# Cross-attention with a sparse feed-forward on one core: the feed-forward stage of the last group taken a step later

## The reference, cut to what matters

```
def _L0_xattn_ref(...):            # 32 query heads in 8 groups of 4, D = 128
    q, k, v = query @ Wq, key @ Wk, value @ Wv     # then rotary embedding on q and k
    attn = jax.nn.softmax(jnp.where(mask == 0, -1e9, q @ k.T / sqrt(D)), axis=-1)
    return (attn @ v) @ Wo

def _L0_ffn_ref(hidden_states, router_weight, router_bias, expert_bias):
    logits = jnp.einsum('th,eh->te', flat, router_weight) + router_bias
    scores = jax.nn.softmax(logits, axis=-1)       # 64 experts
    topk_w, topk_idx = jax.lax.top_k(scores, 8)
    w_sum = topk_w.sum(axis=-1, keepdims=True)
    w_dense = zeros.at[rows, topk_idx].add(topk_w)
    return flat * w_sum + w_dense @ expert_bias

x = x + _L0_xattn_ref(_layernorm(x), ctx, ctx, ...)
x = x + _L0_ffn_ref(_layernorm(x), ...)
```

## Time and profile before

| | |
|---|---|
| Median of 3 runs | 610.95 us (610.76 to 611.58) |
| The profiled execution | 615.61 us, its span 613.7 us |
| Busy in the span | PE 586.2 us (96%), DVE 479.1 (78%), POOL 423.8 (69%), ACT 396.0 (65%) |
| Granted clock of PE | 0.985 of full over the span; 0.7 in the last of 40 slices |
| Chain that ended last, by engine | PE 68%, DVE 9%, POOL 7%, issue 6%, ACT 5%, DMA 3% |

### The profile page before, as it was taken

The page is one execution under the profiler, slowest core; times in us unless marked ns, Lnnn a source line. Parts: engine busy times, 40 slices in busy tenths (PEclk is TensorE's granted clock), DMA queues, the critical chain, the costliest instruction groups (busy, mean ns, idle before and its releaser), DMA issues.

```text
span 613.7 us, 10554 instructions
## 1 busy us (share of the span) xinstructions
PE 586.2 (96%) x2980; PEld 490.4 (80%) x2980; DVE 479.1 (78%) x792; ACT 396.0 (65%) x1054; POOL 423.8 (69%) x390
## 2 busy tenths in 40 slices
PE   8989889898999999999999999999999999999886
PEld 7867778677888888888888888888888888777674
DVE  5667986777778687877977798778787876977886
ACT  5236454767767777677776777767767776775443
POOL 5466588879687787868868886787787763664231
PEclk9989999998999999999999999999999999999997
DMA  8965324210321301121012111111310030000001
GB/s 289 347 186 138 97 104 152 88 35 15 107 68 36 88 23 64 51 85 51 17 52 85 51 51 49 54 68 34 102 36 33 17 86 18 19 18 1 36 34 71
DMA packets 30817, 45.40 MB, mean 74 GB/s; under 512 B 3008, under 2 KB 11328, under 8 KB 30784
## 3 DMA queue, kind: packets, MB, share of 16 engines
q1 hardware_dynamic: 30256, 43.95, 22.6%
q0 software_dynamic: 384, 1.05, 0.5%
q10 hardware_dynamic: 144, 0.00, 0.0%
HBM read 35.03 MB, written 9.96 MB: 73 GB/s over the span
## 4 chain that ended last, share of the span: by engine, by line
PE 68%; DVE 9%; POOL 7%; issue 6%; ACT 5%; DMA 3%; SPq 2%; DVEq 0%; ACTq 0%; POOLq 0%
PE outp L1614 8%; PE score L1595 8%; PE outp L1616 8%; PE outp L1615 8%; PE bank_a L1467 4%; PE bank_a L1469 4%; PE bank_a L1468 4%; PE probT L1627 4%; POOL rot L495 3%; DMA v_dram<-v_stage 2%; PE attnT L1453 2%; PE bank_c L1469 2%; PE bank_c L1468 2%; PE attnT L1455 2%; PE attnT L1454 2%
## 5 line engine op out<-in xcount | busy, mean ns | idle before, releaser
L495 POOL TENSOR_TENSOR rot<-rot,sinT 128x512 f32<-128x512 f32 x80 | 110.5, 1382 | 51.4 <-ACT rot L742 51.2
L908 ACT ACTIVATE probs<-score,negmax 128x128 f32<-128x128 f32 x256 | 90.7, 367 | 29.2 <-DVE negmax L1241 29.2
L615 POOL TENSOR_TENSOR probs<-probs,rsum 128x512 f32<-128x512 f32 x64 | 69.3, 1083 | 45.6 <-DVE rsum L1247 45.6
L1614 PE MATMUL outp<-wo_hi,oT_hi 128*128 128x512 f32 x240 | 95.5, 398 | 2.1 <-DVE oT_lo L1266 1.3
L1616 PE MATMUL outp<-wo_hi,oT_lo 128*128 128x512 f32 x240 | 93.8, 391 | 0.0
L1615 PE MATMUL outp<-wo_lo,oT_hi 128*128 128x512 f32 x240 | 93.5, 390 | 0.0
L1254 DVE TENSOR_TENSOR resid<-resid,outp 128x512 f32<-128x512 f32 x60 | 41.0, 684 | 54.4 <-PE outp L1616 54.4
L1093 DVE TENSOR_TENSOR qT<-qT,rot 128x512 f32<-128x512 f32 x57 | 69.9, 1230 | 4.0 <-POOL rot L495 1.6
L1595 PEld LDWEIGHTS score<-kT,qT 128*128 128x128 f32 x512 | 67.6, 193 | 5.5 <-DVE qT L1093 0.6
L1595 PE MATMUL score<-kT,qT 128*128 128x128 f32 x512 | 68.3, 277 | 0.2 <-DVE qT L1093 0.2
L916 ACT ACTIVATE pT_hi<-probT 128x512 fp32r<-128x512 f32 x64 | 38.3, 598 | 42.2 <-PE probT L1627 41.8
(11 more groups left out here) (297 smaller groups left out, 1513.2 us busy)
## 6 DMA issues: line engine op xcount, KB each, us to landing
ring_b<-in_wo SPq DMA_DIRECT2D x32, 256.0 KB
ring_a<-in_wq SPq DMA_DIRECT2D x28, 256.0 KB, 2.7
v_dram<-v_stage SPq DMA_DIRECT2D x16, 256.0 KB, 3.5
v_raw<-v_dram SPq DMA_DIRECT2D x16, 256.0 KB, 2.6
k_dram<-k_stage SPq DMA_DIRECT2D x14, 256.0 KB, 2.1
kT<-k_dram SPq DMA_DIRECT2D x14, 256.0 KB, 2.8
ctx_in<-in_ctx SPq DMA_DIRECT2D x8, 256.0 KB, 4.1
ring_b<-in_wv SPq DMA_DIRECT2D x8, 256.0 KB
```

What stands on the lines that cost most here:

```text
L495: pool.tensor_tensor(rot[:, k0 % 2, :], rot[:, k0 % 2, :], sinT[:, half * W:(half + 1) * W], ALU.mult).then_inc(sin_done, 1)
L615: pool.tensor_tensor(probs[:, p], probs[:, p], rsum[:, p, :].unsqueeze(2).broadcast_to([P, GH, S]), ALU.mult).then_inc(soft_done, 1)
L908: last = act.activation(probs[:, p, h, :], heads(score[p][:, :])[:, h, :], ACT.Exp, bias=negmax[:, p, h:h + 1], accum_out=sums[:, p, h:h + 1])
L1614: pe.matmul(ps[:, :], oT_hi[:, cols], w[0], start=h == 0, stop=False)
```

## The change

The feed-forward is the same, instruction for instruction; the last group's order changes on PE, DVE, ACT and POOL, three instructions of blocks 0 to 4 go from DVE to POOL, and banks are dealt out otherwise.

- PE: ffn_logits(b-3) stands between the scores and the transposes of step b, one step later than before; the kept transpose is that of block b-4 and stands ahead of output; ffn_mix is that of block b-4 at the step's end. ffn_xT stays where it was.
- DVE: ffn_max(b-3) and, from step 5, ffn_out(b-5) come behind lo_p. After accumulate the order is invert_sums, ffn_keep(b-3), ffn_stats(b-1), lo_o.
- ACT: the exponentials of the attention come ahead of ffn_exp(b-3) and ffn_xT(b-2).
- POOL: soften comes ahead of the feed-forward's part, and a new ffn_split(b-3) does ff_kept and ff_split for blocks 0 to 4.
- Block 4 mixes in score[0]; the logits of block 6 go to bank_a.

The diff, cut to its core:

```diff
-        mixes = [bank_b] * (B - 2) + [score[1], attnT]
-        logit_bank = [bank_a] * (B - 2) + [score[0], probT]
+        mixes = [bank_b] * (B - 4) + [score[0], bank_b, score[1], attnT]
+        logit_bank = [bank_a] * (B - 1) + [probT]
...
@@ POOL
+            def ffn_split(b):
+                pool.wait_ge(f_rest, b + 1)
+                if b >= 1:
+                    pool.wait_ge(f_klo, b)
+                pool.tensor_tensor(ff_kept[:, :], ff_exp[:, b % FF, :], ff_rest[:, b % FF, :], ALU.subtract).then_inc(f_kept, 1)
+                pool.wait_ge(f_kept, b + 1)
+                if b >= 1:
+                    pool.wait_ge(f_keptT, b)
+                pool.tensor_copy(ff_split[:, 0, :], ff_kept[:, :]).then_inc(f_khi, 1)
+                pool.wait_ge(f_khi, b + 1)
+                pool.tensor_tensor(ff_split[:, 1, :], ff_kept[:, :], ff_split[:, 0, :].bitcast(F32), ALU.subtract).then_inc(f_klo, 1)
...
@@ ACT
-                if part == 0 and b >= 3:
-                    ffn_kept(b - 3)
-                if part == 0 and b >= 2:
+                if part == 0 and b >= 4:
+                    ffn_kept(b - 4)
+                if part == 1 and 3 <= b < B - 1:
+                    ffn_exp(b - 3)
+                if part == 1 and b >= 2:
                     ffn_xT(b - 2)
-                if part == 0 and b >= 3:
-                    ffn_scale(b - 3)
-                if part == 1 and b >= 2:
+                if part == 2 and b >= 4:
+                    ffn_scale(b - 4)
+                if part == 2 and b == B - 2:
                     ffn_exp(b - 2)
...
@@ DVE
-                if part == 0 and b >= 3:
+                if part == 0 and 3 <= b < B - 1:
+                    ffn_max(b - 3)
+                if part == 0 and b >= 5:
+                    ffn_out(b - 5)
+                if part == 1 and b >= 3:
                     ffn_keep(b - 3)
                 if part == 1 and b >= 1:
                     ffn_stats(b - 1)
-                if part == 2 and b >= 2:
+                if part == 2 and b == B - 2:
                     ffn_max(b - 2)
-                if part == 2 and b >= 3:
-                    ffn_out(b - 3)
...
@@ DVE, ffn_keep, behind the kept sum
+                if b < B - 3:
+                    return
...
@@ PE
+                if last:
+                    ffn(b, 1)
...
-                if part == 0 and b >= 2:
+                if part == 0 and 3 <= b < B - 1:
+                    ffn_logits(b - 3)
+                if part == 1 and b >= 4:
+                    ffn_kept(b - 4)
+                if part == 2 and b >= 2:
                     ffn_xT(b - 2)
-                if part == 0 and b >= 3:
-                    ffn_kept(b - 3)
-                if part == 1 and b >= 2:
+                if part == 3 and b >= 4:
+                    ffn_mix(b - 4)
+                if part == 3 and b >= B - 2:
                     ffn_logits(b - 2)
-                if part == 1 and b >= 3:
-                    ffn_mix(b - 3)
...
-                elif b < B - 2:
-                    pe.wait_ge(f_out, b)
-                elif b == B - 2:
+                elif mixes[b] == bank_b:
+                    pe.wait_ge(f_out, b if b < B - 4 else b - 1)
+                elif b < B - 1:
                     pe.wait_ge(exp_done, STEPS)
@@ PE, behind the loop
+                if h == 2:
+                    ffn_mix(B - 4)
...
+            ffn_kept(B - 4)
             output(B - 1, STEPS - 1, False, False, KV - 1, True, tail)
```

More of the change, by code:

```diff
@@ L684, in step @@
                     pool.tensor_tensor(ff_eb_lo[:, :], ebias[:, :], ff_eb_hi[:, :].bitcast(F32), ALU.subtract).then_inc(f_eblo, 1)
+                if not (last and b + FIRST >= B):
+                    soften(b % 2, n + FIRST + 1)
                 if last:
                     ffn(b)
-                if not (last and b + FIRST >= B):
-                    soften(b % 2, n + FIRST + 1)
             def ffn(b):
+                if 3 <= b < B:
+                    ffn_split(b - 3)
                 if b >= 3:
@@ L1071, in _ @@
                 step(KV - 1, b, last=True)
+            ffn_kept(B - 4)
+            ffn_exp(B - 3)
+            ffn_scale(B - 4)
             ffn_xT(B - 2)
@@ L1329, in step @@
                     row_max(b % 2, n + FIRST + 1)
+                lo_p(n, first and b == 0)
                 if last:
                     ffn(b, 0)
-                lo_p(n, first and b == 0)
                 if b in ROPES and (b == 0 or not last):
@@ L1338, in step @@
                     accumulate((b - 1) % B, n, first, last and b > 0)
+                if ahead:
+                    invert_sums(b % 2, n + FIRST + 1)
                 if last:
                     ffn(b, 1)
-                if ahead:
-                    invert_sums(b % 2, n + FIRST + 1)
                 if not last:
@@ L1406, in ffn_keep @@
                 dve.reciprocal(ff_rsum[:, b % FF:b % FF + 1], ff_sum[:, b % FF:b % FF + 1]).then_inc(f_rsum, 1)
-                dve.wait_ge(f_rest, b + 1)
-                dve.tensor_tensor(ff_kept[:, :], exp, rest, ALU.subtract).then_inc(f_kept, 1)
                 if b >= 1:
@@ L1411, in ffn_keep @@
                 dve.tensor_reduce(ff_kept_sum[:, :], ff_top[:, :], X_AXIS, ALU.add).then_inc(f_ksum, 1)
+                if b < B - 3:
+                    return
+                dve.wait_ge(f_rest, b + 1)
+                dve.wait_ge(f_klo, b)
+                dve.tensor_tensor(ff_kept[:, :], exp, rest, ALU.subtract).then_inc(f_kept, 1)
                 dve.wait_ge(f_kept, b + 1)
@@ L1436, in _ @@
                 step(KV - 1, b, last=True)
+            ffn_max(B - 3)
+            ffn_out(B - 5)
             ffn_keep(B - 3)
+            ffn_out(B - 4)
             ffn_max(B - 2)
@@ L1621, in step @@
                     scores(b + FIRST, g)
+                if last:
+                    ffn(b, 0)
                 pe.wait_ge(soft_done, n + 1)
@@ L1646, in step @@
                             m7(4, g)
+                if last:
+                    ffn(b, 1)
                 if not (first and b == 0):
-                    output((b - 1) % B, n - 1, first and b == 1, b == 1, g, last and b > 0, (lambda h: ffn(b, 0) if h == GH - 1 else None) if last else None)
+                    output((b - 1) % B, n - 1, first and b == 1, b == 1, g, last and b > 0, (lambda h: ffn(b, 2) if h == GH - 1 else None) if last else None)
                 pe.wait_ge(pt_lo, n + 1)
```

10 lines of the change are left out of this document (5 added, 5 removed).

## The result

The changed kernel takes 620.0 us (median of 4 runs, 619.21 to 620.19) against 610.88 for the kernel before in the same measurement: 1.0132 times as long, 95% interval 1.0098 to 1.0165. Its profiled execution took 619.21 us, with a span of 617.4.

The account below looks back on a forecast made before the run. Neither PE nor DVE was full; PE waited at the kept transpose for DVE's split. A new ring of waits, net +5.2 us, plus 4.5 for the clock gave +9.7 on the median 610.95: 620.6 us, range 618 to 623.

Parts of the forecast that it names:

- The ring: Steps 5 to 7: kept transpose waits for DVE's ffn_out, accumulate for PE's output; accumulates 10.31, 8.98 and 9.94 us apart.
- Steps 0 to 4: Start of the last group: faster; accumulate of block 2 at 562.94, step 4 takes 7.18 us against 8.69 now.
- POOL: POOL's three split instructions: 0.43 us each with the wait, just covered in step 4, so 0; other end 3.6 us.
- The clock: PE idles 3.2, 2.9 and 3.8 us in steps 5 to 7; half clock follows, 1.5 us each, 4.5 us.
- Three falls in three idle times of 2 us and more: Argument from the earlier trace against the clock holding: idle times of 1.98 and 2.42 us and one between were each followed by half clock.
- A part may fall into it and cost nothing: After a longer PE idle time, part of the 3.4 us at half speed may lie inside it; 1.5 us taken, not 1.7.
- Rival 1: PE's clock holds, or falls inside the gaps of steps 5 to 7: 616.1 us, chance 0.18.
- To the last accumulate: Last distance: 6.96 now, + 0.70 for ffn_keep ahead of oT_lo + 0.55 for a ffn_mix inside output = 8.21 us.
- The sum: Whole kernel: +5.2 + 4.5 = +9.7 us, the profiled execution going from 615.61 to 625.3.
- From the profile to the median: Median of the runs shown is 4.7 us below the profiled execution; the same difference turns 625.3 into 620.6 us.
- POOL dear: POOL dear for 64 columns; its split, not ffn_out, ends last in step 4 and at the end: 624.2 us, chance 0.07.
- Faster: Steps 5 to 7: ffn_out not last, ending within 3.3 us of accumulate; 607.8 us, chance 0.11.

Follow-up runs that it names:

- the second run: Changed kernel with 11 matmuls that nothing reads on PE ahead of the kept transpose in steps 5, 6 and 7: 615.88 us, ratio 1.0069.
- its three variants with the ring unfilled: Changed kernel with the split back on DVE (626.35 us), that with ffn_stats ahead of ffn_keep (625.94 us), and changed kernel with an extra POOL instruction per split (620.64 us).
- the delay: Changed kernel with one more POOL instruction of 128x512, read by nothing, ahead of each split of blocks 0 to 4: 620.64 us in one execution.
- The version above: Changed kernel with ffn_mix(b-4) inside output, ffn_scale(b-4) ahead of ACT's exponentials, ffn_out(b-4) behind DVE's ffn_max(b-3): 608.56 us, ratio 0.9952 to the kernel before.

## Why the prediction was right

Predicted 620.6 us, measured 620.0, for the reason given. That the two lie within 0.6 us is in part luck: the terms were 1.1 us too large in the last group. Step by step:

- **The ring.** Right in place, releaser and size. From accumulate to ff_out's end 6.62 was summed for step 5 and 6.46 measured, PE idles 3.17, 2.93 and 3.75 us where 3.2, 2.9 and 3.8 stood. Without the clock the second run gives 10.08, 8.95 and 9.77 for the 10.31, 8.98 and 9.94 of the sum.
- **Steps 0 to 4.** 6.48 and 7.18 predicted, 6.38 and 6.91 measured. The terms were charged too dear where rows of before carried another pair of instructions: accumulate costs 0.61 us when the reciprocal follows (564.69 to 565.30), not the 0.72 it takes ahead of ffn_stats.
- **POOL.** Not on the path in step 4, as predicted, and 0.98 us for the three instead of 1.29: the single prices (0.24 and 0.32) were near the 0.3 on the line, but the wait for the one before, charged at 0.13 each, is 0.07 and 0.08 between them (559.96 to 560.03, 560.27 to 560.35), and none behind the last.
- **The clock.** 4.5 us predicted, 4.6 measured by filling the gaps. The size held; one of its two reasons did not. "Three falls in three idle times of 2 us and more" was partly the luck of one execution: in the profile after, the same idle times of the head were followed by none. Nor was the idle time of 1.77 us that none followed a bound: idle times of 1.44, 1.48 and 1.77 us ahead of the first transposes were followed by one in three of the later traces. With the gaps of the ring a fall came every time, twelve times in four traces, in seven of them inside the gap and in five up to 1.2 us behind the restart. "A part may fall into it and cost nothing" held for a small part only: in step 7 the fall came 0.15 us inside the gap, and that stretch cost 1.44 us where the other two cost 1.58 and 1.56. Where it came 0.74 us or more inside, in three gaps of other runs, the stretch was twice as long (below), so that the cost went up. The low end of my range, 2.4 us for the three, has nothing in the runs to support it; and its upper end, 623, is more than its terms give (610.95 + 5.2 + 5.1 + 0.5 = 621.8). The Trainium skill (TensorE: Matmul & The Clock Gate, What's actually happening) has the clock fall after an idle interval and lets the intervals run freely, not with the kernel; with idle times near 2 us, which are followed by a fall in one execution and not in another, the second half agrees. Rival 1, for which the strict reading of the first half spoke, did not come true: a fall came with each of the three gaps.
- **To the last accumulate.** 8.21 predicted, 7.88 measured. ffn_keep ahead of oT_lo adds 0.59 (accumulate at 598.07 and its 0.61, ffn_stats at 599.27) and not 0.70; the rest of the 0.33, in the mix and output, I did not take apart.
- **The sum.** +9.7 predicted; the distances give +8.64 and the medians +9.1. All terms together were 1.06 us too large: 0.10, 0.27, 0.15, −0.03, 0.23 and 0.33 in the six distances. Behind the last accumulate, put at nothing, it was 0.12. The medians' 9.1 is closer to the forecast than the distances are.
- **From the profile to the median.** I took the 4.7 us between them as a constant. It was not: it was the three half-clock stretches of the head, which the profiled execution of after did not have (619.21, below its median). Taking the difference between orders from the trace and the level from the medians was what kept this from doing harm.
- **The rivals.** Clock holds: refuted by the trace of the changed kernel, three stretches in three gaps, and by those of its three variants with the ring unfilled. POOL dear: refuted by the delay, which steps 5 and 6 do not feel. Faster: its point of decision, ff_out within 3.3 us of accumulate, was right as a condition. The version above, in which ff_out comes ahead of accumulate, is that case, and measured 608.56 where the rival said 607.8.

## What to carry to other kernels

When an instruction is moved, ask first which buffer it frees, and who waits for that with the most work queued behind it: one 0.7 us read of a shared bank, placed behind its engine's other duties, tied two engines, each busy for 7.2 us of an old step's 8.7, into a ring in which each idled for the other. Put such a reader where its engine waits anyway. A wait of 3 us on PE is to be charged with the half clock that came with it in all twelve cases here: 1.5 us more each, and 1.3 on top of that where the stretch was the longer one (12.51 against 11.21).

Compare orders by distances between fixed points of the trace, and levels by medians of many executions; a single profiled execution can lie 5 us off. When idle time is filled, look in the trace whether the filling landed in it.

## What the runs showed of the hardware beyond this

- Whether a half-clock stretch follows an idle time of 1.4 to 2.4 us in the head differs from one execution to the next of the same code: behind 1.44, 1.48, 1.77, 1.98 and 2.42 us one came, behind 1.41, 1.73 and 2.41 none. Block 1's accumulate comes at 550.9 to 551.6 us with no stretch in the unfilled head, at 553.1 to 554.6 with two and at 556.5 to 557.6 with three. In the last group none came behind 1.78 and 2.08 us.
- A stretch at 0.50 came in two lengths, 3.4 and 6.8 us. In the four kernels with the ring, PE restarted 0.74, 0.81 and 2.14 us after the fall in the three long ones (the delayed POOL's last, and one in each of the two with the split on DVE). In the nine short ones it restarted 0.4 to 1.2 us before the fall (five) or up to 0.7 us after it (four). The idle time itself did not decide: 3.76, 3.89 and 4.49 us belong to the long ones, 2.93 to 4.39 us to the short ones. A gap that contains the fall by 0.74 us or more was dearer here, not cheaper.
- 128x64 on POOL: 0.32 us for a subtraction, 0.24 for a cast. On DVE 0.22 and 0.20. One small instruction costs POOL 0.04 to 0.10 us more than DVE; at 128x512 it was 1.04 against 0.69.
- A DVE instruction that reads two SBUF operands can stretch from 0.22 to 0.72 us beside POOL's soften; ff_shift, also 128x64, took 0.51 to 0.86 beside it in the old order, and 0.27 or 0.28 where the change put it.
